# Scores computed turned, with their maxima in a padding row; two output buffers; half of each output product on GpSimd

## What is computed

```
def step(h, inp):                         # the selective scan, D_INNER 384, D_STATE 16
    dA  = exp(dt_t[..., None] * A)
    dBu = (dt_t * u_t)[..., None] * B_t[:, None, :]
    h = dA * h + dBu
    y = einsum('bdn,bn->bd', h, C_t)      # the product with C, then the sum over the states
...
q, k, v = heads(layernorm(x) @ w_qkv)     # 12 heads of 16
a = softmax(einsum('bhnd,bhmd->bhnm', q, k) * 16 ** -0.5, axis=-1)
o = einsum('bhnm,bhmd->bhnd', a, v) @ w_proj + b_proj
...
h = gelu(layernorm(x) @ w1 + b1) @ w2 + b2   # the small block adds three channel-masked variants by gates
```

## Time and profile before

| | us |
|---|---|
| median of 3 runs | 6029.06 (5992.82 to 6056.17) |
| profiled execution, its own time | 6015.9 |
| span of the profiled execution | 6014.1 |
| VectorE busy | 4949.1 (82%) |
| TensorE busy | 4481.5 (75%) |
| ScalarE busy | 3542.3 (59%) |
| GpSimd busy | 1.5 |
| mean granted TensorE clock | 0.803 of full |
| DMA | 953.98 MB, 159 GB/s on average |

### The profile page before, as it was taken

The page is one execution under the profiler, slowest core; times in us unless marked ns, Lnnn a source line. Parts: engine busy times, 40 slices in busy tenths (PEclk is TensorE's granted clock), DMA queues, the critical chain, the costliest instruction groups (busy, mean ns, idle before and its releaser), DMA issues.

```text
span 6014.1 us, 72139 instructions
## 1 busy us (share of the span) xinstructions
PE 4481.5 (75%) x24044; PEld 2601.8 (43%) x24044; DVE 4949.1 (82%) x3709; ACT 3542.3 (59%) x7970; POOL 1.5 (0%) x9
## 2 busy tenths in 40 slices
PE   4677777777777777777777777777777777777787
PEld 2344444444444444444444444444444444444444
DVE  4988898888889788988988889787888878877871
ACT  2456665556666555666656676565666656655553
POOL 0000000000000000000000000000000000000000
PEclk7788888778788888887888888887888888877775
DMA  5887777777768677776876776766767677665740
GB/s 138 195 184 175 165 163 170 161 165 182 168 150 186 156 157 181 178 163 155 184 169 146 179 177 150 160 152 152 176 148 162 150 165 165 153 157 136 169 101 2
DMA packets 182851, 953.98 MB, mean 159 GB/s; under 512 B 26557, under 2 KB 76157, under 8 KB 84042
## 3 DMA queue, kind: packets, MB, share of 16 engines
q1 hardware_dynamic: 182442, 948.83, 69.0%
HBM read 888.14 MB, written 60.60 MB: 158 GB/s over the span
## 4 chain that ended last, share of the span: by engine, by line
PE 39%; DVE 27%; issue 16%; ACT 10%; DMA 7%; SPq 1%; DVEq 1%; ACTq 0%; POOL 0%; POOLq 0%
DVE hs L1047 11%; DMA out<-h 6%; PE f_ps L658 5%; PE f_ps L647 4%; DVE hs L1036 3%; PE y_ps L470 3%; PE f_ps L546 3%; DVE neg_max L1141 3%; PE f_ps L572 3%; PE f_ps L612 3%; PE a_ps L516 3%; DVE hs L1053 2%; PE f_ps L555 2%; ACT decay L799 2%; PE f_ps L592 2%
## 5 line engine op out<-in xcount | busy, mean ns | idle before, releaser
L1047 DVE TENSOR_TENSOR_SCAN hs<-decay,hs 128x2192 f32<-128x2192 f32 x384 | 1810.7, 4715 | 0.1
L799 ACT ACTIVATE decay<-decay,a_cols 128x273 f32<-128x273 f32 x3072 | 1386.1, 516 | 0.4
L1036 DVE TENSOR_TENSOR hs<-hs,b_ps 128x2192 f32<-128x2192 f32 x384 | 929.7, 2421 | 16.7 <-DMA hs<-dtu_rows 16.7
L1053 DVE TENSOR_TENSOR hs<-hs,c_s 128x2192 f32<-128x2192 f32 x384 | 933.9, 2432 | 10.4 <-issue 10.4
L599 PE MATMUL f_ps<-ident,hid 92*92 92x92 f32 x3456 | 490.1, 291 | 447.7 <-ACT hid L885 447.7
L506 PE MATMUL a_ps<-xn,w_in_s 96*128 96x274 f32 x1536 | 529.0, 474 | 286.0 <-ACT xi L822 186.1
L599 PEld LDWEIGHTS f_ps<-ident,hid 92*92 92x92 f32 x3456 | 360.0, 147 | 635.7 <-ACT hid L885 568.7
L470 PE MATMUL y_ps<-hs,y_pick 128*32 128x274 f32 x6144 | 553.7, 489 | 32.8 <-DVE hs L1053 32.8
L885 ACT ACTIVATE hid<-f_ps,neg_max 92x274 f32<-92x274 f32 x1152 | 463.7, 481 | 170.7 <-DVE neg_max L1141 170.4
L1141 DVE TENSOR_REDUCE neg_max<-f_ps 92x4 f32<-92x1096 f32 x288 | 370.3, 1286 | 226.1 <-PE f_ps L592 226.1
L506 PEld LDWEIGHTS a_ps<-xn,w_in_s 96*128 96x128 f32 x1536 | 321.9, 223 | 475.4 <-ACT xi L822 241.6
(11 more groups left out here) (133 smaller groups left out, 5617.4 us busy)
## 6 DMA issues: line engine op xcount, KB each, us to landing
decay<-dt_rows SPq DMA_DIRECT2D x384, 1096.0 KB, 10.5
hs<-dtu_rows SPq DMA_DIRECT2D x384, 1096.0 KB, 13.9
dt_rows<-dt SPq DMA_DIRECT2D x192, 137.0 KB, 10.4
dtu_rows<-dtu SPq DMA_DIRECT2D x192, 137.0 KB, 10.5
xp<-in_patches SPq DMA_DIRECT2D x32, 588.0 KB, 18.3
out<-h SPq DMA_DIRECT2D x32, 205.5 KB, 11.3
h<-in_txt SPq DMA_DIRECT2D x32, 57.8 KB, 2.3
w_in_s<-in_w_in SPq DMA_DIRECT2D x1, 1152.0 KB
```

The costliest lines, as they stand in the source:

```text
L799: e = act.activation(dec[:, k, t], dec[:, k, t], ACT.Exp, scale=a_cols[:, d * IC + u, TILES * half + k:TILES * half + k + 1])
L1036: dve.tensor_tensor(x[:, :, :], x[:, :, :], b_ps[:, 0:T].unsqueeze(1).broadcast_to([128, TILES, T]), ALU.mult).then_inc(dbu_done, 1)
L1047: dve.tensor_tensor_scan(i, a, i, 0.0, ALU.mult, ALU.add).then_inc(scan_done, 1)
L1053: dve.tensor_tensor(x[:, :, :], x[:, :, :], c_s[d][:, :].unsqueeze(1).broadcast_to([128, TILES, T]), ALU.mult).then_inc(hc_done, 1)
```

## The change

Three parts.

1. **Turned scores.** `row_maxima` writes the negated maxima into column 16 of each head's 32 columns of `neg_max` (zero elsewhere), so that a matmul with `ident_4` (4 times the identity) lays them into a padding row of the q tile: `q_with_maxima` (new) sums three such matmuls and the q product in bank 4, `maxima_copy` (new, ScalarE) copies that with the scale 1/4 over q, and k has a 1 in the same row (`k_one` as bias). `turned_scores` (new) then multiplies k as weights by q and gets scores less their maxima, already turned; `softmax_exp` is one instruction per step, from the four banks into `prob_t`. Transposes, `turn_copy` and `prob` go. q and k are kept per group (`qk[0..2]`, two of them in the room of `prob`). The new table `SLOTS` puts scores ("s") and turned scores ("t") one per gap, from gap 10 to 27; each waits for the reader of the slot before it. `MAX_GAPS` are the gaps of `q_with_maxima`.
2. **Two output buffers** `h2[0..1]`: `add_mixer` waits for the store of the batch before the one whose buffer it would have waited for.
3. **GpSimd** multiplies tiles 4 to 7 of each half unit's states by C as soon as its scan is done, VectorE tiles 0 to 3 in the old place. `sum_states` and `c_copy` wait for both.

```diff
-        h2 = sb("h2", [CH, 2, T])
+        h2 = [sb(f"h2_{i}", [CH, 2, T]) for i in range(2)]
...
-        qk = sb("qk", [128, 2, T])
+        qk_0 = sb("qk_0", [128, 2, T])
...
-        prob = hid[0:QT, 12:16, :]
-        neg_max = sb("neg_max", [QT, 4])
+        qk = [qk_0, hid[:, 12:14, :], hid[:, 14:16, :]]
+        neg_max = sb("neg_max", [QT, 2, 3, 128])
+        ident_4 = sb("ident_4", [QT, QT])
+        k_one = sb("k_one", [128, 1])
...
+        POOL_TILE = 4
...
-        V_GAPS = (10, 11, 12)
+        V_GAPS = (9, 10, 10)
+        Q_GAPS = (11, 12)
         STEPS = 3 * GROUPS
-        SCORE_GAPS = [10 + 2 * s for s in range(STEPS)]
-        TURN_GAPS = [gap + 1 for gap in SCORE_GAPS]
-        Q_GAPS, K_GAPS = (14, 20), (15, 21)
-        AV_GAPS = (16, 22, 28)
-        SUM_GAPS = (17, 23, 28)
-        INV_GAPS = (18, 24, 28)
-        NORM_GAPS = (18, 24, 29)
+        SLOTS = [("s", 0, 0), ("s", 0, 1), ("s", 0, 2), ("s", 1, 0), ("t", 0, 0), ("s", 1, 1), ("t", 0, 1),
+                 ("s", 1, 2), ("t", 0, 2), ("s", 2, 0), ("t", 1, 0), ("s", 2, 1), ("t", 1, 1), ("s", 2, 2),
+                 ("t", 1, 2), ("t", 2, 0), ("t", 2, 1), ("t", 2, 2)]
+        SLOT_GAP = 10
+        MAX_GAPS = (13, 18, 24)
+        AV_GAPS = (19, 25, 28)
+        SUM_GAPS = (20, 26, 28)
+        NORM_GAPS = (21, 27, 29)
         PROJ_GAP = 30
         FC1_GAPS = (34, 35)
...
-                sp.dma_start(out[number(b)], h2[:, :, :]).then_inc(out_stored, 16)
+                sp.dma_start(out[number(b)], h2[parity(b)][:, :, :]).then_inc(out_stored, 16)
...
+            def output_product(b, q):
+                d, x = q // 6, hs[q % 4][:, POOL_TILE:TILES, :]
+                pool.wait_ge(c_copied, at(b, 2, d + 1))
+                pool.wait_ge(scan_done, at(b, SCANS, q + 1))
+                pool.tensor_tensor(x, x, c_s[d][:, :].unsqueeze(1).broadcast_to([128, TILES - POOL_TILE, T]),
+                                   ALU.mult).then_inc(hc_pool, 1)
+
+            def step(b, f, e, a):
+                for q in range(SCANS):
+                    output_product(b, q)
+
+            program(step, pool.Fori, lambda: None, lambda f, e: None)
...
+                wait(pe, hc_pool, at(b, SCANS, q + 1))
...
-                elif s == 0:
+                elif (g, s) == (1, 0):
                     pe.wait_ge(v_copied, at(f, 3, 3))
-                    wait(pe, o_norm, at(f, GROUPS, g - 1))
                 else:
-                    pe.wait_ge(qk_copied, at(f, 2 * GROUPS, 2 * g + 1))
+                    pe.wait_ge(qk_copied, at(f, 2 * GROUPS, 2 * g + s))
...
+            def q_with_maxima(f, g):
+                pe.wait_ge(nmx_done, at(f, STEPS, 3 * g + 3))
+                if g == 0:
+                    pe.wait_ge(qk_copied, at(f, 2 * GROUPS, 2 * GROUPS))
+                if g == 1:
+                    pe.wait_ge(mx_copied, at(f, GROUPS, 1))
+                if g == 2:
+                    pe.wait_ge(o_norm, at(f, GROUPS, 1))
+                for t in range(3):
+                    new = min(t, 1)
+                    pe.matmul(f_ps[:, 4, QS[t] + new:QS[t] + QT], neg_max[:, g % 2, t, :], ident_4[:, new:QT],
+                              start=True, stop=False, skip_group_check=True)
+                for i in range(2):
+                    mm = pe.matmul(f_ps[:, 4, 0:T], w_qk_s[:, i, 0, g * 128:(g + 1) * 128], cen[:, i, :],
+                                   start=False, stop=(i == 1), skip_group_check=True)
+                mm.then_inc(mx_mm, 1)
 
             def v_mms(f, t):
...
-            def scores(f, s):
-                g, t = s // 3, s % 3
+            def after_slot(f, n):
+                if n > 0:
+                    kinds = [kind for kind, _, _ in SLOTS[:n]]
+                    pe.wait_ge(nmx_done if kinds[-1] == "s" else pexp, at(f, STEPS, kinds.count(kinds[-1])))
+
+            def scores(f, g, t):
                 pe.wait_ge(qk_copied, at(f, 2 * GROUPS, 2 * g + 2))
-                if s > 0:
-                    pe.wait_ge(pt_copied, at(f, STEPS, s))
+                after_slot(f, SLOTS.index(("s", g, t)))
                 for r in range(4):
                     rows = slice(32 * r, 32 * r + 32)
-                    pe.matmul(f_ps[0:QT, r, 0:T], qk[rows, 0, QS[t]:QS[t] + QT], qk[rows, 1, :],
+                    pe.matmul(f_ps[0:QT, r, 0:T], qk[g][rows, 0, QS[t]:QS[t] + QT], qk[g][rows, 1, :],
                               start=True, stop=True).then_inc(sc_mm, 1)
 
-            def turn(f, s):
+            def turned_scores(f, g, t):
+                pe.wait_ge(mx_copied, at(f, GROUPS, g + 1))
+                after_slot(f, SLOTS.index(("t", g, t)))
                 for r in range(4):
-                    pe.wait_ge(pexp, at(f, 4 * STEPS, 4 * s + r + 1))
-                    for k in range(3):
-                        mm = pe.transpose(f_ps[0:QT, r, k * QT:(k + 1) * QT],
-                                          prob[:, r, QS[k]:QS[k] + QT], ident[0:QT, 0:QT])
-                    mm.then_inc(pt_mm, 1)
+                    rows = slice(32 * r, 32 * r + 32)
+                    pe.matmul(f_ps[0:QT, r, 0:T], qk[g][rows, 1, QS[t]:QS[t] + QT], qk[g][rows, 0, :],
+                              start=True, stop=True).then_inc(tr_mm, 1)
 
             def av(f, g):
-                pe.wait_ge(pt_copied, at(f, STEPS, 3 * g + 3))
+                pe.wait_ge(pexp, at(f, STEPS, 3 * g + 3))
                 if g < GROUPS - 1:
-                    pe.wait_ge(qk_copied, at(f, 2 * GROUPS, 2 * g + 4))
+                    pe.wait_ge(mx_copied, at(f, GROUPS, g + 2))
                 else:
                     pe.wait_ge(o_norm, at(f, GROUPS, g))
...
+                wait(act, hc_pool, at(b, SCANS, 6 * d - 6))
...
-                wait(act, sc_mm, at(f, 4 * STEPS, 12 * g))
-                act.activation(qk[:, 0, :], f_ps[:, bank, 0:T], ACT.Copy, scale=-HD ** -0.5).then_inc(qk_copied, 1)
+                wait(act, tr_mm, at(f, 4 * STEPS, 0))
+                act.activation(qk[g][:, 0, :], f_ps[:, bank, 0:T], ACT.Copy, scale=-HD ** -0.5).then_inc(qk_copied, 1)
 
             def k_copy(f, g, bank):
                 act.wait_ge(qk_mm, at(f, 2 * GROUPS, 2 * g + 2))
-                act.activation(qk[:, 1, :], f_ps[:, bank, 0:T], ACT.Copy).then_inc(qk_copied, 1)
+                act.activation(qk[g][:, 1, :], f_ps[:, bank, 0:T], ACT.Identity, bias=k_one[:, 0:1])\
+                    .then_inc(qk_copied, 1)
+
+            def maxima_copy(f, g):
+                act.wait_ge(mx_mm, at(f, GROUPS, g + 1))
+                act.wait_ge(sc_mm, at(f, 4 * STEPS, 12 * g + 12))
+                act.activation(qk[g][:, 0, :], f_ps[:, 4, 0:T], ACT.Copy, scale=HD ** -0.5).then_inc(mx_copied, 1)
 
             def v_copy(f, t):
...
-            def softmax_exp(f, s):
-                act.wait_ge(nmx_done, at(f, STEPS, s + 1))
-                wait(act, pt_mm, at(f, 4 * STEPS, 4 * s))
-                for r in range(4):
-                    act.activation(prob[:, r, :], f_ps[0:QT, r, 0:T], ACT.Exp, scale=-1.0,
-                                   bias=neg_max[:, r:r + 1]).then_inc(pexp, 1)
-
-            def turn_copy(f, s):
-                g, t = s // 3, s % 3
+            def softmax_exp(f, g, t):
+                act.wait_ge(tr_mm, at(f, 4 * STEPS, 4 * (3 * g + t) + 4))
                 if t == 0:
                     wait(act, av_mm, at(f, GROUPS, g))
-                act.wait_ge(pt_mm, at(f, 4 * STEPS, 4 * s + 4))
-                new = min(t, 1)
-                act.activation(prob_t[:, :, :, QS[t] + new:QS[t] + QT],
-                               f_ps[0:QT, 0:4, 0:3 * QT].rearrange("p r (k t) -> p r k t", k=3)[:, :, :, new:],
-                               ACT.Copy).then_inc(pt_copied, 1)
+                act.activation(prob_t[:, :, t, :], f_ps[0:QT, 0:4, 0:T], ACT.Exp).then_inc(pexp, 1)
 
             def av_copy(f, g):
...
-                dve.tensor_tensor(x[:, :, :], x[:, :, :], c_s[d][:, :].unsqueeze(1).broadcast_to([128, TILES, T]),
+                x = x[:, 0:POOL_TILE, :]
+                dve.tensor_tensor(x, x, c_s[d][:, :].unsqueeze(1).broadcast_to([128, POOL_TILE, T]),
                                   ALU.mult).then_inc(hc_done, 1)
...
-                wait(dve, out_stored, at(f, 16, 0))
+                wait(dve, out_stored, at(ago(f, 1), 16, 0))
...
-            def row_maxima(f, s):
-
-                dve.wait_ge(sc_mm, at(f, 4 * STEPS, 4 * s + 4))
-                wait(dve, pexp, at(f, 4 * STEPS, 4 * s))
-                dve.tensor_reduce(neg_max[:, 0:4], f_ps[0:QT, 0:4, 0:T], AX_X, ALU.min).then_inc(nmx_done, 1)
+            def row_maxima(f, g, t):
+
+                dve.wait_ge(sc_mm, at(f, 4 * STEPS, 4 * (3 * g + t) + 4))
+                wait(dve, mx_mm, at(f, GROUPS, 1 if g == 2 else 0))
+                dve.tensor_reduce(neg_max[:, g % 2, t, :].rearrange("p (r c) -> p r c", r=4)[:, :, HD],
+                                  f_ps[0:QT, 0:4, 0:T], AX_X, ALU.min).then_inc(nmx_done, 1)
...
```

106 lines of the change are left out of this document (63 added, 43 removed).

## The result

The changed kernel takes 6312.35 us (6310.7 to 6315.6), the kernel before on the same chip 6031.27 (5992.82 to 6056.17): 1.0473 times the time (95% interval 1.0417 to 1.0529). The prediction was 5794 us, 4% faster. Even its range, up to 6070, does not hold the result.

The account below looks back on a forecast made before the run. It took a nearly full, in-order VectorE (82% busy) that stops at a few waits as the bound. 6014.1 - 438 - 84 - 76 + 190 + 186 = 5792 us of span, 5794 with 1.8 more; range 5580 to 6070.

Parts of the forecast that it names:

- -438: Output product: VectorE does half of each of 384 products and gets 438 us lighter.
- A microsecond off VectorE is worth a microsecond, unless one of these waits comes next.: VectorE, nearly full: work taken off it shortens the time equally, unless one of its listed waits swallows the saving.
- GpSimd contention: full block less the absorbed part, +186: VectorE instructions with two SBUF inputs behind six scans a batch stand until GpSimd finishes: 5.8 us a batch, +186 us.
- Attention: I take a third off, -76: VectorE's 226.1 us of waits for scores before the row maxima shrink by a third, -76 us.
- doubled: Upper bound for the 226.1 us of waits before the maxima; the lower bound was that they are gone.
- rival of crowded score gaps: Score gaps set the pace: four waits of 2.5 us a batch, +170, 5964 us; chance 0.16.
- TensorE +4: Attention on TensorE: transposes removed, turned scores, q products and maxima matmuls added, net +4 us of busy time.
- Given back: rstd 56, fc2 62, o_s 73: VectorE's waits set by other engines' chains grow by what VectorE saved ahead of them, together +190 us.
- Second buffer -84: At add_mixer, the 83.6 us of VectorE's waits for the store of h2 go, -84 us.

Follow-up runs that it names:

- e2: The kernel before with only the split of the output product, half of it on GpSimd; 6272.2 us.
- e4: The kernel before with only the turned scores; 6277.1 us.
- e3: The kernel before with only the second output buffer (two h2); 5918.3 us.
- e6: The kernel before with VectorE multiplying only tiles 0 to 3 by C and nobody the other four; 6004.4 us.
- e5: The kernel before with GpSimd's half, and VectorE's input product moved ahead of taps and dt sums at five scan gaps; 6087.7 us.
- e1: The changed kernel with the whole output product back on VectorE (turned scores and two output buffers stay); 6237.9 us.
- e9: The kernel of e7 with ScalarE's exponential of gap 26 ahead of the silu and its two table loads; 6206.3 us.
- e7: The changed kernel without GpSimd's half, TensorE issuing the scores of gaps 10, 15, 17, 19, 21 and 23 first in their gap; 6206.1 us.
- e11: Turned scores and two output buffers without GpSimd's half, all maxima and their score matmuls left out, nine slots two gaps apart; 5522.3 us.
- e10: The kernel before with every transpose issued twice; 6135.6 us.
- e8: The kernel before with two output buffers and 28 unused matmuls a batch added where TensorE waits; 5949.2 us.
- e13: The kernel of e11 with VectorE multiplying only tiles 0 to 3 by C, the other four left unmultiplied; 5497.7 us.

## Why the prediction was wrong

Set beside the runs of each part alone, its terms are these: for GpSimd's half -438 + 190 + 186 = -62 us, measured +248 (e2); for attention -76, measured +253 (e4); for the second buffer -84, measured -106 (e3). So two terms have the wrong sign, and they miss by over 300 us each. Step by step, as it put them:

- **"A microsecond off VectorE is worth a microsecond, unless one of these waits comes next."** This is the step that failed first. The -438 was right as busy time and worth 6 us as time (e6), which is within the noise. The prediction had 190 us of it given back at rstd, fc2 and o_s (56, 62 and 73); in e6 these three took 38, 56 and 43. What it left out is the rest: the maxima, where it had counted on a gain, wait 461.0 us instead of 226.1, and the store 115.4 instead of 83.6. 82% of busy time did not make VectorE the bound. The chain of the earlier trace rows, with 27% of VectorE and 39% of TensorE, had said as much, and the prediction read it as "no single engine's" without drawing the sum from it.
- **"GpSimd contention: full block less the absorbed part, +186."** The lock is there and its gross size was nearly right: some 273 us of longer instructions against 291 estimated. The taps have 182 of it as estimated, the dt sum 72; the scaling of xn, which the prediction counted in, kept its 715 ns, and a bias sum, which it did not name, has 20. But the cost is not set against a saving, since there was none. In the kernel before, e2 lies 268 us above e6, which differs only in GpSimd's half (4.4% of the kernel before, which each was timed beside). e5 takes the block away by order alone: 216 us of VectorE's time go and 185 us of time, close to the 186 that the prediction had left after absorption; where the rest was absorbed was not measured. The other 83 us between e5 and e6 are not the lock, and their cause is open. In the changed kernel the third part costs only 74 us net (e1 to after). That the blocked instructions (taps, dt sum) stand ahead of hand-overs to ScalarE and TensorE would explain why they count where the shortened product does not; no run isolates it. The two pages of the Trainium skill that the prediction weighed held. SBUF — State Buffer, "Who interferes with whom", names the instruction with two SBUF inputs as one that contends with GpSimd and the one with a PSUM input as free, and the rows show 820 ns for the taps (504 before) and 2421 for the input product (2421 before). GPSIMD Engine Reference, "Performance versus the Vector engine", has 4497 ns for 2048 elements, from which the prediction's estimate of 2.4 us for the half came. The rows have 2.37, and the sum took 2.1.
- **"Attention: I take a third off, -76."** Wrong in sign: the waits before the maxima grew by 236 us, to 462.3, the term's own bound of "doubled". Turned scores and buffers make 120 us of that (346.3 in e1), and the rest came with GpSimd's half. The rival of crowded score gaps named the place and priced it at +170 against the forecast; alone, turned scores cost 253 us against the kernel before (e4). The prediction looked at the work between two slots, not at the whole loop. The four banks are filled 18 times a batch in both kernels, once a gap from 10 to 27. Before, each filling waited for ScalarE: the transposes for the exponentials, the next scores for the copy. Now nine of them stand behind a score slot and wait for VectorE's maxima, and six of these nine are turned scores of an earlier group. So TensorE waits for VectorE in the midst of exponentials (374.1 us), with the in-projection and the sums over states queued behind. In e4 TensorE's waits at the fillings are 348.7 us for the maxima and 265.8 for the exponentials, 614 together; before, they were 447.7 and 30.8 for exponentials and copy. The prediction booked the 447.7 as lost waits, "and with them the reason why scores came late"; waits for VectorE took their place.
- **"TensorE +4."** Busy time rose by 94. Turned scores cost 291.4 us and q_with_maxima 300.6 (the sum had 265 and 229); av, the same instructions, went from 208.1 to 284.9 with a mean of 663 ns instead of 509. The mean granted clock fell from 0.803 to 0.767; in the clock rows of the trace the engine stands at the lower of its levels, 1.2 GHz, for 2941 us of the span, and for 2367 before.
- **"Given back: rstd 56, fc2 62, o_s 73."** rstd grew by 48 and fc2 by 67 (29.6 at L1199, 37.0 at L1204), near what was worked out. But 32 of rstd's 48 are there already in e1 (193.7), which has no half product, so the match of rstd is partly luck. o_s grew by 168, and by 133 with turned scores alone (e4). The last group's three turned scores now come one after another in gaps 25 to 27, with silu's table loads between the exponentials, and av, sums and inversion wait behind them; e9, the one try at this tail, moved the wait and did not shorten it.
- **"Second buffer -84."** Right in mechanism and somewhat low: 106 us alone (e3), 39 beside turned scores (e4 to e1).
- **Absent from the sum** was that these terms meet the same waits. The sum took them as independent; the three parts alone come to +253, +248 and -106, +395 together, and in one kernel to +281.

How scores of the last group come late can be followed in the changed kernel's timeline. TensorE in gaps 18 and 19, from the product of q with the maxima to the scores:

```profile
2896.78 1.12 PE L610 MATMUL f_ps<-cen,w_qk_s 96*128 96x274 f32 x2
2897.70 2.03 PE L528 MATMUL a_ps<-xn,w_in_s 96*128 96x274 f32 x4
2899.66 2.97 PE L653 MATMUL f_ps<-hid,v_s 92*32 92x274 f32 x24
2902.40 2.05 PE L492 MATMUL y_ps<-hs,y_pick 128*32 128x274 f32 x16
2904.39 1.24 PE L633 MATMUL f_ps<-hid 32*92 32x274 f32 x8
```

It never pauses here, and the scores come out at 2905.6. VectorE in the same stretch:

```profile
2894.33 4.71 DVE L1095 TENSOR_TENSOR_SCAN hs<-decay,hs 128x2192 f32<-128x2192 f32 x1
2905.86 1.30 DVE L1190 TENSOR_REDUCE neg_max<-f_ps 92x4 f32<-92x1096 f32 x1 [6.81 <-PE f_ps L633]
```

It has finished its scan and waits 6.81 us. e7 moves these scores ahead of the rest of gap 19, and the time hardly changes: the work that was ahead of them then stands behind, and something else is late.

**What stays open.** The runs show that taking the maxima out gives more than either engine's work in them (e11; whether by the maxima themselves or by the nine fillings fewer was not separated), that TensorE's amount of work does not explain e4 (e10), and that neither the place of the scores (e7) nor the order of exponential and silu at one gap (e9) is the cause alone. Most of the 253 us can be seen as two waits of VectorE, before the maxima and before o_s (e4), but how they divide between the waits of score slots for VectorE, the later tail of the last group and the lower clock was not separated. An order of slots that keeps the maxima of one group clear of the turned scores of another was not tried. That the lower clock makes TensorE's chains longer fits the rows of av; e8 raised the clock only at the price of added work, so its share was not measured. And what swallows VectorE's saving even without maxima (e13) is named only by its waits, not traced to one chain.
